# ScalarE's search round without its smallest operation and in another order, and one VectorE round per group handed to ScalarE in the second step

## The reference

```
for s in range(2):
    logits = (Xa @ W1) @ W2 @ (Xa @ W3).T
    # per row: keep the largest softmax values until their sum reaches 0.9
    A  = softmax(where(keep, logits, -inf))
    Xf = Rf @ Xf;  Xb = Rb @ Xb;  Xa = A @ Xa      # Rf, Rb: the adjacency scaled by row and by column
    Z  = Z + Xf @ U1[s] + Xb @ U2[s] + Xa @ U3[s]
```

## Time and profile before

| what | value |
|---|---|
| time, median of 3 runs | 3784.11 us (3783.64 to 3785.8) |
| span of the profiled execution | 3781.4 us, 42418 instructions |
| TensorE busy | 2942.2 us (78%) |
| VectorE busy | 3553.9 us (94%) |
| ScalarE busy | 3150.2 us (83%) |
| first step, VectorE's first round to its last cut | about 71 to 1577 us |
| second step, the same | about 1623 to 3116 us |

### The profile page before, as it was taken

One profiled execution on the slowest core, in us unless ns is written; L12 is line 12 of the kernel. 1 busy time (PEld: TensorE's weight loads), 2 busy tenths in 40 slices (PEclk: granted clock), 3 DMA queues, 4 the chain that ended last, 5 costly groups with the idle time before them and its releaser, 6 DMA issues. The chain is left out here.

```text
span 3781.4 us, 42418 instructions
## 1 busy us (share of the span) xinstructions
PE 2942.2 (78%) x14004; PEld 2083.2 (55%) x14004; DVE 3553.9 (94%) x4740; ACT 3150.2 (83%) x4561; POOL 360.3 (10%) x417
## 2 busy tenths in 40 slices
PE   6568787786878787648879797888979734799998
PEld 4456666575756666413535354453535424567787
DVE  7999999999999999699999999999999996777887
ACT  6999999999999999389999999999999952345443
POOL 3000000000000000000000000000000005434444
PEclk9689888898989888869989898998989867899999
DMA  2112122212222220032111111111111005355553
GB/s 92 64 55 87 61 93 65 94 54 85 71 78 81 67 87 17 29 133 63 35 41 49 37 46 35 54 37 51 37 41 49 21 5 193 111 176 187 195 205 108
DMA packets 157483, 292.05 MB, mean 77 GB/s; under 512 B 14480, under 2 KB 87248, under 8 KB 153936
## 3 DMA queue, kind: packets, MB, share of 16 engines
q1 hardware_dynamic: 128032, 216.33, 18.2%
q10 hardware_dynamic: 29232, 73.02, 5.5%
HBM read 236.34 MB, written 52.95 MB: 77 GB/s over the span
## 5 line engine op out<-in xcount | busy, mean ns | idle before, releaser
L693 DVE SCALAR_TENSOR_TENSOR s_dump<-s_rows,s_mid 128x3327 bf16<-128x3327 f32 x608 | 2238.8, 3682 | 2.3 <-issue 0.7
L642 ACT ACTIVATE s_adump<-s_rows,s_mid 128x3327 int8<-128x3327 f32 x324 | 995.6, 3073 | 10.6
L648 ACT ACTIVATE s_adump<-s_rows,s_mid 128x3327 int8<-128x3327 f32 x324 | 992.0, 3062 | 0.0
L905 PE MATMUL bank<-x,s_slab 128*128 128x512 f32 x1352 | 633.6, 612 | 0.0
L882 PE MATMUL bank<-kh,qs 128*128 128x512 f16 (+1 forms) x364 | 146.9, 404 | 361.6 <-DVE s_rows L672 351.1
L905 PEld LDWEIGHTS bank<-x,s_slab 128*128 128x128 f32 x1352 | 266.4, 198 | 280.8 <-issue 268.9
L949 PE MATMUL bank<-hb,s_wT 128*128 128x256 f32 x1352 | 356.9, 409 | 69.8 <-ACT s_wT L520 69.7
L949 PE MATMUL bank<-xab,s_wT 128*128 128x256 f32 x1352 | 348.6, 402 | 70.5 <-ACT s_wT L520 70.4
L938 PE MATMUL bank<-ident,s_rows 128*128 128x128 f32 x1352 | 230.5, 298 | 187.3 <-DVE s_rows L747 186.5
L905 PE MATMUL bank<-hb,s_slab 128*128 128x257 f32 x1352 | 353.3, 402 | 0.0
L949 PEld LDWEIGHTS bank<-hb,s_wT 128*128 128x128 f32 x1352 | 261.6, 204 | 119.9 <-ACT s_wT L520 54.2
(11 more groups left out here) (180 smaller groups left out, 4713.8 us busy)
## 6 DMA issues: line engine op xcount, KB each, us to landing
s_slab<-adjT_dram SPq DMA_DIRECT2D x104, 448.0 KB, 4.0
s_slab<-adjT_dram SPq DMA_DIRECT2D x104, 384.0 KB, 3.7
e_adj<-adjR_dram ACTq DMA_DIRECT2D x23, 1664.0 KB, 7.3
strip<-adjR_dram SPq DMA_DIRECT2D x52, 448.0 KB, 3.5
strip<-adjR_dram SPq DMA_DIRECT2D x52, 384.0 KB, 3.3
e_ring<-sc_d SPq DMA_DIRECT2D x72, 256.0 KB, 5.9
sc_d<-e_stage SPq DMA_DIRECT2D x60, 256.0 KB, 2.4
su_d<-s_su_out ACTq DMA_DIRECT2D x26, 256.0 KB, 2.0
```

The lines of the kernel that those rows point to most:

```text
L642: nc.scalar.activation(adump[:], row(g, r), ACT.Sign, bias=st(mid, g, 2), accum_out=cnt[:]).then_inc(S["a_eval"], 1)
L648: nc.scalar.activation(adump[:], row(g, r), ACT.Relu, bias=st(mid, g, 2), accum_out=gap[:]).then_inc(S["a_eval"], 1)
L693: nc.vector.scalar_tensor_tensor(out=dump[:], in0=row(g, r), scalar=st(mid, g, r), in1=row(g, r), op0=ALU.is_gt, op1=ALU.mult, accum_out=s ...
L905: ins = nc.tensor.matmul(acc, slab[:, i % NSLAB, j - PIECES[p], :], s_op[:, j, 0:SN], start=False, stop=(j == NT - 1))
```

## The change

In ScalarE's round `Relu` becomes `Abs`, with another constant, so that `base` is no longer needed: `over` is computed from the constant `rest` and the count right after the first pass. The passes now follow each other without a fill between them. Both fills of a round stand at its end, one between `sgn` and `mid`, one between `mid` and the next pass.

VectorE now has tiles 0 and 2 of a group, ScalarE tile 1. The exponential of ScalarE's own next tile stands ahead of its search and no longer in a fill. The other two are filled in at beats 22 and 31. `take` is spread over beats 10 to 37, TensorE's logits over 9 to 36. Tile 1 is cut at beat 2 of the next group.

In the second step (`TAILS[1]`) VectorE does only 18 rounds of tile 2. ScalarE takes the threshold over at the start of the next group (`take_on`), does the 19th round, then the exponential, then begins its own tile. Tile 2 is then cut at beat 5.

```diff
+TAILS = ((0, 0, 0, 0, 0, 0, 0, 0), (1, 1, 1, 1, 1, 1, 1, 1))
...
 def load_order(g):
-    return [r for r in ((1, 0) if g == LAST else (2, 0, 1)) if r in roles(g)]
+    return [r for r in (0, 2, 1) if r in roles(g)]
...
+    LAST_TAKE = 2 * BISECT - 1
+    def tail(g):
+        return TAILS[s][g] if g < LAST else 0
...
+    def first_take(g):
+        return LAST_TAKE - 9 * len(roles(g + 1))
...
+            def take_on(g):
+                act.wait_ge(mid_ready[1], dve_rounds(g + 1, 2))
+                nc.scalar.activation(rest[:, 1:2], st(Z, g, 2), ACT.Copy, scale=2.0 * P_NUC - 1.0).then_inc(S["a_taken"], 1)
+                nc.scalar.activation(less[:, 1:2], st(mid, g, 2), ACT.Copy, scale=-1.0).then_inc(S["a_taken"], 1)
+                act.wait_ge(S["a_taken"], 2 * sum(1 for q in range(g + 1) if tail(q)))
...
-                nc.scalar.activation(base[:], st(mid, g, 2), ACT.Identity, scale=float(N), bias=st(target, g, 2)).then_inc(S["a_base"], 1)
...
+            def search(g, r, it, n, first, second):
...
+                nc.scalar.activation(adump[:], row(g, r), ACT.Sign, bias=low, accum_out=cnt[:]).then_inc(S["a_eval"], 1)
+                nc.scalar.activation(fac[:], low, ACT.Copy, scale=last * (down - up) / 2).then_inc(S["a_fac"], 1)
+                nc.scalar.activation(mean[:], low, ACT.Copy, scale=last * (down + up) / 2).then_inc(S["a_fac"], 1)
+                act.wait_ge(S["a_eval"], 2 * n + 1)
+                nc.scalar.activation(over[:], cnt[:], ACT.Identity, scale=low, bias=rest[:, k:k + 1]).then_inc(S["a_over"], 1)
+                nc.scalar.activation(adump[:], row(g, r), ACT.Abs, bias=low, accum_out=gap[:]).then_inc(S["a_eval"], 1)
+                act.wait_ge(S["a_over"], n + 1)
+                act.wait_ge(S["a_eval"], 2 * n + 2)
+                nc.scalar.activation(sgn[:], gap[:], ACT.Sign, scale=-1.0, bias=over[:]).then_inc(S["a_sgn"], 1)
+                first()
+                act.wait_ge(S["a_sgn"], n + 1)
+                act.wait_ge(S["a_fac"], 2 * n + 2)
+                nc.scalar.activation(st(mid, g, r) if it + 1 == BISECT else low, sgn[:], ACT.Identity,
+                                     scale=fac[:], bias=mean[:]).then_inc(S["a_mid"], 1)
+                second()
+                act.wait_ge(S["a_mid"], n + 1)
...
             def beats(g, h):
                 if g == LAST:
-                    return (2 * h, 2 * h + 1) if h <= NGRP + 3 else (h + NGRP + 4,)
-                return (h,)
+                    lead = 2 * tail(LAST - 1)
+                    twice = 3 * NGRP + 1 - lead
+                    if h < lead:
+                        return (h,)
+                    b = lead + 2 * (h - lead)
+                    return (b, b + 1) if b <= 3 * NGRP else (h + twice // 2,)
+                return due(h, 0, 2 * (BISECT + (tail(g - 1) if g else 0)), 2 * BISECT)
...
+                if g >= 1:
+                    if tail(g - 1):
+                        take_on(g - 1)
+                    for it in range(BISECT - tail(g - 1), BISECT):
+                        search(g - 1, 2, it, act_rounds(g) - BISECT + it, next_fill, next_fill)
+                    exponent(3 * g + len(roles(g)) - 1)
+                begin(g)
+                for it in range(FIRST_PART if g == LAST else BISECT):
+                    search(g, 1, it, act_rounds(g) + it, next_fill, next_fill)
...
                 if g >= 1 and b == 2:
+                    cut(g - 1, 1)
+                if g >= 1 and b == 2 * tail(g - 1) + 3:
                     cut(g - 1, 2)
...
-                        for n in due(b, 34 - 9 * loads, 34, NCH * loads):
+                        for n in due(b, first_take(g) - 1, LAST_TAKE - 1, NCH * loads):
                             logits(3 * NCH * (g + 1) + n)
```

More of the change, by code:

```diff
@@ L389, in layer_step @@
             sb(tag + n, [P, 6], F32) for n in ("nb", "Z", "target", "mid", "hit", "mass", "kept", "rk"))
-        cnt, gap, base, over, sgn, fac, mean = (sb(tag + n, [P, 1], F32) for n in ("cnt", "gap", "base", "over", "sgn", "fac", "mean"))
+        cnt, gap, over, sgn, fac, mean = (sb(tag + n, [P, 1], F32) for n in ("cnt", "gap", "over", "sgn", "fac", "mean"))
+        rest, less = (sb(tag + n, [P, 2], F32) for n in ("rest", "less"))
         u12 = sb(tag + "u12", [P, KC, 2 * D], F32)
@@ L494, in sides, with begin @@
-            def sides(g, it):
+            def begin(g):
+                act.wait_ge(S["exp_done"], LOADS.index((g, 1)) + 1)
+                if g >= 1:
+                    act.wait_ge(S["a_mid"], act_rounds(g))
+                nc.scalar.activation(rest[:, 0:1], st(Z, g, 1), ACT.Copy, scale=2.0 * P_NUC - 1.0).then_inc(S["a_begun"], 1)
+                nc.scalar.activation(less[:, 0:1], st(Z, g, 1), ACT.Copy, scale=-LEAST * 2.0 ** LOG_STEP).then_inc(S["a_begun"], 1)
+                act.wait_ge(S["a_begun"], 2 * g + 2)
@@ L495, in sides @@
                 up, down = rate(it)
                 last = -1.0 if it + 1 == BISECT else 1.0
-                nc.scalar.activation(base[:], st(mid, g, 2), ACT.Identity, scale=float(N), bias=st(target, g, 2)).then_inc(S["a_base"], 1)
[L498 to L502, removed]
+                low = less[:, k:k + 1]
@@ L620, in fill @@
                 if g + 1 < TRIPLES:
[L621 to L623 removed]
+                    for p in range(len(roles(g + 1)) - 1):
+                        if b == first_take(g) + 12 + 9 * p:
+                            exponent(3 * (g + 1) + p)
             def fill_end(r, b):
@@ L637, in _, with next_fill @@
             for g in range(TRIPLES):
-                r, rounds = (1, FIRST_PART) if g == LAST else (2, BISECT)
-                begin(g, r)
-                for it in range(rounds):
-                    n = BISECT * g + it
-                    nc.scalar.activation(adump[:], row(g, r), ACT.Sign, bias=st(mid, g, 2), accum_out=cnt[:]).then_inc(S["a_eval"], 1)
-                    sides(g, it)
-                    for b in beats(g, 2 * it):
-                        fill(g, b)
-                    above(g, n)
-                    act.wait_ge(S["a_eval"], 2 * n + 1)
-                    nc.scalar.activation(adump[:], row(g, r), ACT.Relu, bias=st(mid, g, 2), accum_out=gap[:]).then_inc(S["a_eval"], 1)
-                    for b in beats(g, 2 * it + 1):
-                        fill(g, b)
-                    settle(g, n)
-            for b in range(2 * FIRST_PART + NGRP + 4, 2 * BISECT):
+                half = 0
+                def next_fill():
+                    nonlocal half
+                    for b in beats(g, half):
+                        fill(g, b)
+                    half += 1
+                if g >= 1:
+                    if tail(g - 1):
[6 more added lines that the diff above has]
+                    search(g, 1, it, act_rounds(g) + it, next_fill, next_fill)
+            for b in range(beats(LAST, half - 1)[-1] + 1, 2 * BISECT):
                 fill(LAST, b)
```

132 lines of the change are left out of this document (75 added, 57 removed).

## The result

The changed kernel takes 3885.6 us (median of four runs, 3883.6 to 3887.5), the kernel before in the same comparison 3784.6: a ratio of 1.027 [1.025, 1.028], 101 us slower. The forecast was 3860 us, +76. The profiled execution took 3887.5 us, 1.9 over the median; its span is 3885.7 us, 104.3 more than before. 26.8 of these lie in the first step (VectorE's second step starts at 1649.09 instead of 1622.27 us), 74.3 between there and `take_over` of the second step, 3.2 behind that.

What follows compares the result with a forecast made beforehand. VectorE and ScalarE were both taken as full at about 170 us a group, TensorE without slack, ScalarE the bound afterwards. 3784.1 + 65 (second step) + 11 (first step) = 3860 us, range 3808 to 3890.

Steps and rivals of the forecast that it cites:

- What bounds the kernel: Second step's whole groups: VectorE full at 170.0 us, ScalarE needing 168.8; after the change ScalarE 172.4, VectorE 166.2.
- The Abs pass: ScalarE's round: Abs costed like the Sign pass, 3.07 us; without `base` (0.19) a round without a fill takes 7.53 us.
- Fills in pairs and late: Second step's whole groups: ScalarE waits 5 us more a group (0 to 10), 177.4 in all; VectorE waits some 11.
- Four in a row in the last group: Second step's last group: third and fourth evacuations lose 1.7 to 2.2 us each, 16 in all; first step also 16.
- the slow clock: TensorE at 1.2 GHz in each group's first two pairs and the last group's rounds; left out of the sum.
- The first step: Whole groups keep their length; only the last group gets longer, by 11 us, between -1 and +23.
- TensorE hidden: Rival: ScalarE is the bound but without extra waits for TensorE, groups of 172.4 us, 3800 us; chance 0.19.
- Waits feed each other: Rival: TensorE slow at group starts, 10 us a group and 26 in each last group, 3915 us; chance 0.09.
- VectorE as the bound: Rival: VectorE stays the bound at 166.2 us a group and the change is faster, 3753 to 3764 us; chance 0.06.
- a lead of ScalarE that lasts some groups: Rival: `take_on` costs little and early groups' gains offset the rest, near 3784 us; chance 0.04.

Runs made afterwards that it cites:

- run 4: The kernel before with only `base` left out of ScalarE's round and Abs for Relu: 3784.9 us, ratio 1.000 to before.
- run 6: The changed kernel with TensorE doing only the last block of each half of the second step's adjacency product: 3848.5 us, ratio 1.017 to before.
- run 2: The changed kernel with ScalarE's two fills of a round put back at their old places, handed round kept: 3811.5 us, ratio 1.007 to before.
- run 1: The changed kernel with no VectorE round handed to ScalarE in the second step, new fill order kept: 3864.4 us, ratio 1.021 to before.
- run 11: The changed kernel with six extra unread matmuls at five places of each step's last group: 3871.6 us, ratio 1.023 to before.
- 7: The changed kernel with most of the second step's adjacency product left out and no round handed to ScalarE: 3825.6 us, ratio 1.010 to before.

## Why the prediction was right, and where it was off

**What bounds the kernel.** Right. That ScalarE was as full as VectorE, behind a share of 83%, was the reading on which all rests: run 4 shows VectorE as the bound before. After, ScalarE's group less its waits for transposes is 177.6 - 5.2 = 172.4 us in the changed kernel, the very number of the forecast, and 172.5 - 0.6 = 171.9 in run 6. VectorE's list, in run 2, is 166.0 for a forecast of 166.2.

**The Abs pass.** Costed as Sign's 3.07 us; it takes 3058 ns. `base` is worth its start to start and nothing at the end: the new round without a fill, from 2344.73 to 2352.24, is 7.51 us for a forecast of 7.53.

**Fills in pairs and late.** 5 us a group taken, 5.2 measured; the group 177.4 against 177.6; VectorE's chunks 11 against 11.4 a group; the first evacuation 18.4 us behind ScalarE's start of the handed round (2166.53 to 2184.86 is 18.3) and 13.7 behind VectorE's first pass (14.1 in the first whole group, 14.9 in the third). The sum is right, and its mechanism in the main: all 20 waits of the seven groups fall on the second evacuation of a pair. How they come to 5 is in part luck. The prediction had 0.6 to 0.8 us in each of eight pairs and chose 5 between bounds of 0 and 10; the trace has some three waits a group, of 0.3 to 4.2 us, most of them at the seventh and the ninth pair. Nor are the two causes additive as written: with pairs alone the waits are 8.2 us a group (run 1), with the handed round alone 1.2 (run 2).

**Four in a row in the last group.** This is the term that was mis-sized: 16 us of waits in either step. Measured are 24.0 over nine waits in the first step and, by line from 3065 to 3175 us, in the second:

```profile
L550 ACT ACTIVATE s_wT<-bank 128x512 f32<-128x512 f32 (+1 forms) x20 | 10.7, 558 | 23.2 <-PE bank L1000 23.2
```

The prediction gave the third and fourth evacuation 1.7 to 2.2 us each, by the earlier trace rows, which are at a granted clock of 1.00 (1549 to 1553 us). Here the third of a round waits 1.6 to 4.0. The step that failed was to leave the slow clock out of the sum "since these beats have room"; that holds for the start of a group (in the whole groups no evacuation of the first two pairs waits), not for the last one, where little else feeds TensorE. Of the 7.2 us that the second step waits beyond the 16, run 11 takes 6.3 away, and 4.2 of the 8.0 in the first; there the first round kept its wait of 4.0 us, since the extra matmuls came behind the slow products and not ahead of them. The second step's last group from ScalarE's `begin` to `take_over` was 110.4 us; the sum had 102.9, and with the extra matmuls it is 104.1. Of the 74.3 us of the second step 58.0 stand at that `begin` (56.6 forecast) and 16.3 behind it (8.8 forecast).

**The first step.** Whole groups 172 us, as before, and no change but in the last group: right. +11 was forecast, +26.2 came, past the bound of +23. Beside the 8 us of the last paragraph ScalarE waits 5.7 us for an item's transposes, which the sum did not have, and it begins its last group 2.4 us later and not 1: 15 us together. The last of these is no finding: runs 1, 6 and 7, with the same work in the first step, begin that group at 1435.6 to 1436.1 us where this profile has 1439.1, and their `take_over` comes 21.4 to 22.7 us late, just inside the bound. The 18.8 us that VectorE waits at the item's low part are the same delay seen from its side. `take_over` was to wait 5 to 15 us here and 10 to 25 in the second step. It waits 7.3 here, but only because 18.8 are waited ahead of it; VectorE's 26.0 in both steps are the same miss. Run 2 brings all of it back (last group 93.6).

**The rivals.** "TensorE hidden", 3800 us, given 0.19, would have needed TensorE's room; run 6 shows its mechanism in the whole groups once the room is made (172.5 us for 172.4), not in the last one. "Waits feed each other" was near in its 26 us of a last group (23 to 24 measured) and wrong in its 10 us a group. The other two fell with the group length: VectorE as the bound would have had 166.2 us a group, and a lead of ScalarE that lasts some groups would have shown in the first ones, but the first of the seven already takes 179.3 us and none is under 174.7.

## What to carry to other kernels

Before a round of work moves from the fullest engine to another, read the other's need per stage, by its period less its waits, and not its share of the span: here 168.8 of 170 us stood behind 83%. Work that feeds a third engine should be issued evenly: two evacuations side by side, or four, save next to nothing on their own engine (by the prediction's estimate 1 us of 172 here) and cost waits on all three, most where the third is full or falls to its slow clock in between. Room that is real can be used in portions: a handed round in every second group of the first step gained 3.5 us each, in every group of the second it lost.

## What was not expected of the hardware

Idle TensorE time ahead of a burst cost twice in this chain, where TensorE and ScalarE wait for each other in turn: the eight 128x256 f32 products behind a wait of 4.00 us ran at a granted clock of 0.54 and took 3.46 us instead of 1.89, and with 30 extra matmuls in each step's last group the kernel was 14 us faster. The Trainium skill, "TensorE: Matmul & The Clock Gate", section "HAM oscillation — how this bites in real kernels", describes the same for waits on transfers. The trace agrees, with ScalarE's evacuations in the transfers' place.
